# An eight-core linear attention and FFN kernel: the transposed tile is copied out of PSUM by VectorE instead of ScalarE, and the two large weights are loaded last

## The chip, the cores and the metric
The kernel runs on 8 cores of one Trainium2 chip, four on each die. Every core runs the same program on its own sequence. The time is device microseconds of the slowest core. Three runs of the kernel before are shown; the profile is of one further execution.

## The reference
The input x has 8 sequences of 4096 tokens with 1024 values. One core has one sequence.

```
xn = layernorm(x)
# attention: 8 heads of 64, phi(u) = elu(u) + 1, gamma = sigmoid(decay_log)
q, k = phi(xn @ W_Q.T), phi(xn @ W_K.T);  v = xn @ W_V.T
S = gamma*S + k v^T;  z = gamma*z + k         # over the tokens
y = (S^T q) / (z.q + 1e-6) * sigmoid(xn @ W_g.T + b)
s = y @ W_O.T
# spiking FFN
h = relu(xn @ W_fc.T)**2;  y = h @ W_proj.T   # 4096 wide
mem = 0; five times: reset = mem > 1
    mem = 0.9*mem + y - reset;  spikes += mem > 1
out = x + s * silu(spikes / 5)
```

## The kernel before
**Tiles.** A sequence is cut into 32 chunks of 128 tokens, and two chunks make a supertile; there are 16. All weights stay in SBUF as bf16. The normalised and transposed input of a supertile lies in `XR`: 1024 values in eight blocks of 128 rows, and in each block the 128 columns of chunk 0 and those of chunk 1.

**Order.** Each engine runs a program that is written out in order, with semaphore waits between the engines. `Eng.op` puts a drain ahead of an operation that reads or writes what an earlier one of its engine has written since the last drain (or writes what one has read); it does so by the name of the tile. TensorE's program has no drains. `inc` marks the operations that others can wait for.

**A supertile.** For each of its two chunks TensorE makes q in PSUM bank pb2 (L423), k in pb3, the gate in pb2 and v in pb3, then the attention products; VectorE and ScalarE do the element work between them. During this GpSimd loads the x tile that comes two chunks later (`load_xt`), and `emit_A_stats` forms its sums on ScalarE (L298 to L304) and its mean and deviation on GpSimd. Then comes the FFN: 32 blocks of fc products into pb2 or pb3, relu on ScalarE (L661), squaring on VectorE (L666), pj products into pb4, pb5, pb0 and pb1. Then the output projection of chunk 0 into pb2 and pb3.

**The spikes.** `spike_group` handles two of the four banks of y. The even bank's five threshold steps are Sign operations of ScalarE (L747), the odd bank's five are comparisons on VectorE (L752); TensorE adds them up with identity products, even and odd in turn. ScalarE then takes a Tanh of either sum (L781), and VectorE makes the gate out of it (L786, L790).

**Around the change.** The end of a supertile is issued in this order:

```python
        spike_group(0, 1)
        wo1_doh0()
...
            emit_A_xn(c0 + 2, 0)     # place A
        spike_group(2, 3)
        wo1_doh1()
        if sti + 1 < nst:
            emit_A_xn(c0 + 3, 1)     # place B
...
        emit_combine(0, c0, xg_st, spk_s_tail, spk_g_tail)
```

`emit_A_xn` prepares a chunk of the next supertile: ScalarE normalises the x tile into `XF` (L366), TensorE transposes it in eight blocks into the PSUM tile `pbT` (L374), and eight copies of 128 columns bring it into `XR` (L382). The two calls are named place A and place B here; the last supertile has neither. `emit_combine` multiplies s (in pb2 and pb3 for chunk 0) by the gate on VectorE (L809), adds x on GpSimd (L818) and stores. The same for chunk 1 is put off into the next supertile. The q projection of a supertile's first chunk waits for the multiplications of the chunk two before, which read pb2 and pb3:

```python
                E_pe.wait(E_v, combine_mul[c0 - 2])
                E_pe.wait(E_s, xnte_done.get(ch, 0))
```

**The start.** GpSimd issues the loads of all weights, f32 in HBM and bf16 in SBUF, fc and pj (8 MB each in SBUF) ahead of four projections and wo (1 MB each), and the first two x tiles after them. SP issues ten small loads of constants. ScalarE and VectorE work out decay masks from the constants. TensorE's first projection waits for all seven weights.

Of the kernel before, what the change touches and what calls it, by code (L numbers as in the profile page):

```python
# [8 lines left out]
AF = mybir.ActivationFunctionType  # L9
# [3 lines left out]
P = 128  # L13
# [5 lines left out]
CH = 128  # L19
# [70 lines left out]
def build_program(T):  # L90
# [7 lines left out]
    wq_d = dt_("wq", [P, 8 * FH], F32, kind="ExternalInput").ap()  # L98
    wk_d = dt_("wk", [P, 8 * FH], F32, kind="ExternalInput").ap()
    wv_d = dt_("wv", [P, 8 * FH], F32, kind="ExternalInput").ap()  # L100
    wg_d = dt_("wg", [P, 8 * FH], F32, kind="ExternalInput").ap()
    wo_d = dt_("wo", [P, 4 * D], F32, kind="ExternalInput").ap()
    fc_d = dt_("fc", [P, 8 * FF], F32, kind="ExternalInput").ap()
    pj_d = dt_("pj", [P, 32 * D], F32, kind="ExternalInput").ap()
# [13 lines left out]
    wq = S_("wq_sb", [P, 8 * FH], BF16)  # L118
    wk = S_("wk_sb", [P, 8 * FH], BF16)
# [59 lines left out]
                            tile_position=tp)  # L179
        return E_pe.op(f, reads=reads, writes=writes, inc=inc)  # L180

    for w_sb, w_dr in [(fc, fc_d), (pj, pj_d), (wq, wq_d), (wk, wk_d),
                       (wv, wv_d), (wg, wg_d)]:
        E_gp.dma(w_sb[:], w_dr, "wt")
    E_gp.dma(wo[:], wo_d, "wt")

    for dst, src in [(identb[:], identb_d), (tsc, tsc_d), (zmask, zmask_d),
                     (r1t, r1_d), (r127[:], r127_d), (sel[:], sel_d),
# [83 lines left out]
                scalar1=G128B[r_ * DKH:(r_ + 1) * DKH, h:h + 1]),  # L272
                reads=("SCRB", "G128B"), writes=("GDEC",), inc=(p_ == 3 and r_ == 1))

    E_pe.wait(E_gp, ("wt", 7), dma=True)
    E_pe.wait(E_v, c_ssb0)

    xt_cnt = {}
# [80 lines left out]
    def emit_A_xn(ch, cc):  # L359
        buf = XT[ch % 2]  # L360
        key = f"XT{ch % 2}"
        st_ = stats
        rcol = 8 if ch % 2 == 0 else 14
        ncol = 9 if ch % 2 == 0 else 15
        E_s.wait(E_gp, xnstat_done[ch])
        c_xn = E_s.op(lambda e, b=buf, rcol=rcol, ncol=ncol: e.activation(  # L366
            XF[:], b[:], AF.Identity, scale=st_[:, rcol:rcol + 1],
            bias=st_[:, ncol:ncol + 1]),
            reads=(key, "stats"), writes=("XF",), inc=True)
        xnact_done[ch] = c_xn  # L370
        gp_guard["s"] = c_xn
        E_pe.wait(E_s, c_xn)
        for dk in range(8):
            c_T = E_pe.op(lambda e, dk=dk: e.transpose(pbT[:, dk * P:(dk + 1) * P],  # L374
                                                       XF[:, dk * P:(dk + 1) * P],
                                                       identb[:]),
                          reads=("XF", "identb"), writes=("pbT",), inc=(dk == 7))
        xntp_done[ch] = c_T
        E_s.wait(E_pe, c_T)
        for dk in range(8):  # L380
            col = dk * (ST * CH) + cc * CH
            c_ev = E_s.op(lambda e, dk=dk, col=col: e.activation(  # L382
                XR[:, col:col + CH], pbT[:, dk * P:(dk + 1) * P], AF.Identity),
                reads=("pbT",), writes=("XR",), inc=(dk == 7))
        xnte_done[ch] = c_ev

    load_xt(0)
    load_xt(1)
# [22 lines left out]
    for sti in range(nst):  # L411
        c0 = sti * ST
        chunks = [c0, c0 + 1]
        for cc, ch in enumerate(chunks):
            qbank, kbank = pb[2], pb[3]
            if cc == 0:
                E_pe.wait(E_v, combine_mul[c0 - 2])
                E_pe.wait(E_s, xnte_done.get(ch, 0))
            else:
                E_pe.wait(E_s, th_done[ch - 1])  # L420
                E_pe.wait(E_v, vaug_done[ch - 1])
                E_pe.wait(E_s, xnte_done.get(ch, 0))
            for ft in range(4):  # L423
                for dk in range(8):
                    c_qps = mm(qbank[:, ft * P:(ft + 1) * P],
# [115 lines left out]
                          reads=("QF",), writes=("ZP",), inc=True)  # L541
            E_pe.wait(E_v, c_at)
            if cc == 0:
                E_pe.wait(E_s, xnte_done.get(ch + 1, 0))
            for ft in range(4):
                c_kt = E_pe.op(lambda e, ft=ft: e.transpose(
                    pbT[:, ft * P:(ft + 1) * P], KF[:, ft * P:(ft + 1) * P],
# [96 lines left out]
        def emit_fc(ft):  # L644
            bank = pb[2 + ft % 2]
            E_pe.wait(E_v, h2_cnt.get(ft - 2, 0))
            if ft == 0:
                E_pe.wait(E_s, th_c1)
                E_pe.wait(E_v, vaug_c1)
            for dk in range(8):  # L650
                c_fc = mm(bank[:, 0:ST * CH],
                          fc[:, dk * FF + ft * P:dk * FF + (ft + 1) * P],
                          XR[:, dk * ST * CH:(dk + 1) * ST * CH],
                          start=(dk == 0), stop=(dk == 7),
                          reads=("fc_sb", "XR"), writes=(f"pb{2 + ft % 2}",),
                          inc=(dk == 7))
            fc_cnt[ft] = c_fc
            E_s.wait(E_pe, c_fc)
            E_s.wait(E_pe, pj_cnt.get(ft - 2, 0))
            relu_cnt[ft] = E_s.op(  # L660
                lambda e, b=bank, ft=ft: e.activation(H2[ft % 2][:], b[:, 0:ST * CH],  # L661
                                                      AF.Relu),
                reads=(f"pb{2 + ft % 2}",), writes=(f"H2_{ft % 2}",), inc=True)
            E_v.wait(E_s, relu_cnt[ft])
            h2_cnt[ft] = E_v.op(
                lambda e, b=bank, ft=ft: e.tensor_tensor(  # L666
                    out=H2[ft % 2][:], in0=H2[ft % 2][:], in1=b[:, 0:ST * CH],
                    op=ALU.mult),
                reads=(f"H2_{ft % 2}", f"pb{2 + ft % 2}"),
                writes=(f"H2_{ft % 2}",), inc=True)  # L670

        def emit_pj(ft):
# [12 lines left out]
                              inc=(tsub == ST - 1 and doh == 1))  # L685
            pj_cnt[ft] = c_pj

        emit_fc(0)
        emit_fc(1)
        for ft in range(1, 32):  # L690
# [269 lines left out]
```

How the kernel before makes its waits and increments, by code:

```python
            def run(e, fn=fn):  # L52
                fn(e).then_inc(me.sem, 1)
# [17 lines left out]
        def run(e, d=dst_ap, s=src_ap, key=key):  # L71
            e.dma_start(out=d, in_=s).then_inc(me.dsem[key], 16)
# [3 lines left out]
    def wait(self, other, value, dma=False):  # L76
        if dma:
            key, n = value
            if n <= 0:
                return
            o = other
            self.prog.append(lambda e: e.wait_ge(o.dsem[key], n * 16))
        else:
            if value <= 0:
                return
            o = other
            self.prog.append(lambda e: e.wait_ge(o.sem, value))
```

## Time and profile before

| | us |
|---|---|
| runs | 2083.9, 2088.89, 2091.3 (median 2088.89) |
| the profiled execution | 2091.03 |
| its span on the slowest core (core 3) | 2089.5 |
| spans of the eight cores | 2067.4 to 2089.5 |
| TensorE busy | 1552.3 (74%) |
| VectorE busy | 755.5 (36%) |
| ScalarE busy | 668.6 (32%) |
| GpSimd busy | 253.9 (12%) |

The mean granted clock of TensorE was 0.884 on core 3 and 0.884 to 0.893 over the cores. The span runs from the first to the last instruction of a core. In the profile PE is TensorE, PEld its weight loads, DVE VectorE, ACT ScalarE, POOL GpSimd and SP SyncE; a q behind a name is the queue that issues. All products that go through the helper `mm` have the line L178, and are told apart by their tiles. A supertile takes about 119.5 us.

### The profile page before, as it was taken

Reading aid. Unit: us, or ns where it says so; the run is one execution under the profiler, and the core shown is the slowest. Engines: PE = TensorE matmul, PEld = TensorE weight load, DVE = VectorE, ACT = ScalarE, POOL = GpSimd, SP = SyncE. Lnnn points to the kernel's source line nnn. Section 1 sums busy time; section 2 is a strip of 40 time slices with the busy share of each in tenths; the row PEclk is TensorE's granted clock in tenths of the full one; section 3 lists DMA queues with packets and bytes.
Section 4 is the critical chain, followed back from the end, with each engine's and each line's share of the span. In section 5 each row is a group of like instructions: output and inputs, shape, how many; then the busy total and the mean of one; then the engine's idle time right before and its main releaser. Section 6 shows DMA issues by size and latency. Waiting matters only on the chain.

```text
span 2089.5 us, 35959 instructions; the slowest of 8 cores (2067.4 to 2089.5 us)
## 1 busy us (share of the span) xinstructions
PE 1552.3 (74%) x12130; PEld 1035.1 (50%) x12130; DVE 755.5 (36%) x1576; ACT 668.6 (32%) x1497; POOL 253.9 (12%) x843
## 2 busy tenths in 40 slices
PE   0005969778796968779696977879697877969695
PEld 0004646455564646455464645456464645546462
DVE  0013243343425243343524344342534334342433
ACT  0024242423324242432424242332424243242422
POOL 1002011020202011020201102020201102020100
PEclk9998979989898988889798988979798888979898
DMA  9980010010201010010201001020101001020100
GB/s 146 158 131 11 1 36 6 18 24 1 42 1 37 6 33 10 6 37 1 42 1 36 6 20 23 1 41 1 36 6 32 10 6 36 1 42 1 36 1 26
DMA packets 16294, 58.03 MB, mean 28 GB/s; under 512 B 2667, under 2 KB 2676, under 8 KB 14964
## 3 DMA queue, kind: packets, MB, share of 16 engines
q0 software_dynamic: 10480, 38.80, 12.3%
q1 hardware_dynamic: 5636, 16.92, 2.4%
q8 instruction: 103, 1.69, 0.3%
q14 instruction: 75, 0.61, 0.1%
HBM read 77.74 MB, written 16.78 MB: 45 GB/s over the span
## 4 chain that ended last, share of the span: by engine, by line
PE 64%; DVE 9%; ACT 9%; another core or an unknown queue 6%; issue 6%; DVEq 4%; DMA 1%; POOLq 1%; ACTq 1%; POOL 0%; SPq 0%
PE pb L178 63%; DVEq L38 3%; ACT XR L382 2%; DVE MEM L809 2%; ACT SGN L781 1%; ACT SGN L747 1%; ACT XF L366 1%; DVE AT L529 1%; DVE KF L462 1%; DVE VT L502 1%; ACT SCRB L458 1%; ACT KF L456 1%; DVE MEM L786 1%; POOLq L38 1%
## 5 line engine op out<-in xcount | busy, mean ns | idle before, releaser
L178 PE MATMUL pb<-XR,fc_sb 128*128 128x256 bf16 x4096 | 556.4, 282 | 0.0
L178 PE MATMUL pb<-pj_sb,H 128*128 128x512 bf16 x2048 | 536.4, 385 | 5.8 <-DVE H L666 5.7
L178 PEld LDWEIGHTS pb<-XR,fc_sb 128*128 128x128 bf16 x4096 | 413.0, 101 | 164.7 <-issue 5.8
L666 DVE TENSOR_TENSOR H<-H,pb 128x256 bf16<-128x256 bf16 x512 | 215.7, 421 | 666.2 <-ACT H L661 665.2
L661 ACT ACTIVATE H<-pb 128x256 bf16<-128x256 f32 x512 | 196.2, 383 | 738.9 <-PE pb L178 738.9
L178 PEld LDWEIGHTS pb<-pj_sb,H 128*128 128x128 bf16 x2048 | 201.6, 99 | 153.0 <-issue 22.6
L72 POOL DMA_DIRECT2D XF<-x_tok x32 | 18.8, 588 | 1104.2 <-PE pbT L374 1095.1
L178 PE MATMUL pb<-SGN,identb_sb 128*128 128x512 bf16 x192 | 85.2, 496 | 87.2 <-ACT SGN L747 82.0
L178 PE MATMUL pb<-XR,wq_sb 128*128 128x128 bf16 x1024 | 108.8, 302 | 38.4 <-DVE MEM L809 29.9
L178 PEld LDWEIGHTS pb<-XR,wq_sb 128*128 128x128 bf16 x1024 | 101.8, 143 | 41.6 <-issue 40.5
L298 ACT ACTIVATE XF<-XT 128x1024 bf16<-128x1024 bf16 x32 | 33.8, 1056 | 221.9 <-DMA XT<-x_tok 213.2
L818 POOL TENSOR_TENSOR MEM<-MEM,XF 128x512 f32<-128x512 f32 x64 | 74.3, 1162 | 248.5 <-DVE MEM L809 127.4
L752 DVE TENSOR_SCALAR SGN<-pb 128x512 bf16<-128x512 f32 x96 | 66.3, 690 | 81.2 <-PE pb L178 78.2
L178 PEld LDWEIGHTS pb<-SGN,identb_sb 128*128 128x128 bf16 x192 | 19.1, 100 | 150.9 <-issue 150.5
L178 PE MATMUL pb<-lgn,onesr_sb 1*128 1x8 f32 x2 | 0.6, 352 | 121.6 <-ACT lgn L202 121.6
L374 PE MATMUL pbT<-identb_sb,XF 128*128 128x128 bf16 x256 | 20.2, 224 | 87.4 <-ACT XF L366 87.4
L382 ACT ACTIVATE XR<-pbT 128x128 bf16<-128x128 bf16 x256 | 70.9, 277 | 43.9 <-PE pbT L374 28.0
L178 PE MATMUL pb<-XR,wk_sb 128*128 128x128 bf16 x1024 | 81.0, 252 | 0.0
L442 DVE SCALAR_TENSOR_TENSOR QF<-pb,SCRB 128x512 bf16<-128x512 f32 x32 | 22.1, 692 | 157.8 <-ACT SCRB L438 157.8
L178 PEld LDWEIGHTS pb<-XR,wk_sb 128*128 128x128 bf16 x1024 | 78.2, 118 | 0.0
L178 PE MATMUL pb<-wv_sb,XR 128*128 128x512 bf16 x256 | 60.4, 378 | 13.1 <-DVE KF L462 13.1
L178 PE MATMUL pb<-XR,wg_sb 128*128 128x128 bf16 x1024 | 62.3, 219 | 7.3 <-DVE QF L442 7.0
(127 smaller groups left out, 1569.1 us busy)
## 6 DMA issues: line engine op xcount, KB each, us to landing
out<-MEM SPq DMA_DIRECT2D x32, 512.0 KB, 3.3
fc_sb<-fc POOLq DMA_DIRECT2D x1, 8192.0 KB, 58.8
pj_sb<-pj POOLq DMA_DIRECT2D x1, 8192.0 KB, 112.2
XT<-x_tok POOLq DMA_DIRECT2D x32, 256.0 KB, 4.4
XF<-x_tok POOLq DMA_DIRECT2D x32, 256.0 KB, 4.6
wq_sb<-wq POOLq DMA_DIRECT2D x1, 1024.0 KB, 117.8
wk_sb<-wk POOLq DMA_DIRECT2D x1, 1024.0 KB, 123.4
wv_sb<-wv POOLq DMA_DIRECT2D x1, 1024.0 KB, 128.9
```

The source lines that it names most:

```text
L38: self.prog.append(lambda e: e.drain())
L178: return e.matmul(out_ap, lhsT_ap, rhs_ap, start=start, stop=stop, tile_position=tp)
L298: E_s.op(lambda e, b=buf: e.activation(XF[:], b[:], AF.Identity, accum_out=st_[:, 0:1]), reads=(key,), writes=("XF",))
L366: c_xn = E_s.op(lambda e, b=buf, rcol=rcol, ncol=ncol: e.activation(XF[:], b[:], AF.Identity, scale=st_[:, rcol:rcol + 1], bias=st_[:, nco ...
L382: c_ev = E_s.op(lambda e, dk=dk, col=col: e.activation(XR[:, col:col + CH], pbT[:, dk * P:(dk + 1) * P], AF.Identity), reads=("pbT",), wri ...
L442: c_qf = E_v.op(lambda e: e.scalar_tensor_tensor(out=QF[:], in0=qbank[:, 0:FH], scalar=0.0, in1=SCRB[:], op0=ALU.max, op1=ALU.add), reads= ...
L456: E_s.op(lambda e: e.activation(KF[:], kbank[:, 0:FH], AF.Relu, scale=-1.0), reads=("pb3",), writes=("KF",))
L661: lambda e, b=bank, ft=ft: e.activation(H2[ft % 2][:], b[:, 0:ST * CH], AF.Relu),
L666: lambda e, b=bank, ft=ft: e.tensor_tensor(out=H2[ft % 2][:], in0=H2[ft % 2][:], in1=b[:, 0:ST * CH], op=ALU.mult),
L752: vc = E_v.op(lambda e, bufO=bufO, j=j, c=cO: e.tensor_scalar(out=bufO[:, 0:FH], in0=pb[c["bk"]][:, 0:FH], scalar1=THS[j], scalar2=2.0, op ...
L809: c_mul = E_v.op(lambda e, doh=doh, cc=cc, sb_=sb_: e.tensor_tensor(out=OUTB[:, doh * FH:(doh + 1) * FH], in0=sb_[:, 0:FH], in1=G[:, cc * ...
L818: c_comb = E_gp.op(lambda e, doh=doh: e.tensor_tensor(out=OUTB[:, doh * FH:(doh + 1) * FH], in0=OUTB[:, doh * FH:(doh + 1) * FH], in1=XF[: ...
```

## The change
The eight copies of `emit_A_xn` become `tensor_copy` on VectorE, at the same point of the order. ScalarE no longer waits for the transposes; VectorE does. Two waits are added: ScalarE waits for the last transposes before it writes `XF` again, and TensorE waits for VectorE's last copies before it transposes into `pbT` again. TensorE's waits for a finished `XR` name VectorE. At the start fc and pj are issued after the other five weights, still ahead of the x tiles, and count on a semaphore of their own; TensorE's first projection waits for five weights, and the first fc product for these two.

```diff
--- before.py
+++ after.py
@@ -179,10 +179,11 @@
                             tile_position=tp)
         return E_pe.op(f, reads=reads, writes=writes, inc=inc)
 
-    for w_sb, w_dr in [(fc, fc_d), (pj, pj_d), (wq, wq_d), (wk, wk_d),
-                       (wv, wv_d), (wg, wg_d)]:
+    for w_sb, w_dr in [(wq, wq_d), (wk, wk_d), (wv, wv_d), (wg, wg_d)]:
         E_gp.dma(w_sb[:], w_dr, "wt")
     E_gp.dma(wo[:], wo_d, "wt")
+    E_gp.dma(fc[:], fc_d, "wt2")
+    E_gp.dma(pj[:], pj_d, "wt2")
 
     for dst, src in [(identb[:], identb_d), (tsc, tsc_d), (zmask, zmask_d),
                      (r1t, r1_d), (r127[:], r127_d), (sel[:], sel_d),
@@ -272,7 +273,7 @@
                 scalar1=G128B[r_ * DKH:(r_ + 1) * DKH, h:h + 1]),
                 reads=("SCRB", "G128B"), writes=("GDEC",), inc=(p_ == 3 and r_ == 1))
 
-    E_pe.wait(E_gp, ("wt", 7), dma=True)
+    E_pe.wait(E_gp, ("wt", 5), dma=True)
     E_pe.wait(E_v, c_ssb0)
 
     xt_cnt = {}
@@ -363,6 +364,7 @@
         rcol = 8 if ch % 2 == 0 else 14
         ncol = 9 if ch % 2 == 0 else 15
         E_s.wait(E_gp, xnstat_done[ch])
+        E_s.wait(E_pe, gp_guard.get("tp", 0))
         c_xn = E_s.op(lambda e, b=buf, rcol=rcol, ncol=ncol: e.activation(
             XF[:], b[:], AF.Identity, scale=st_[:, rcol:rcol + 1],
             bias=st_[:, ncol:ncol + 1]),
@@ -370,19 +372,22 @@
         xnact_done[ch] = c_xn
         gp_guard["s"] = c_xn
         E_pe.wait(E_s, c_xn)
+        E_pe.wait(E_v, gp_guard.get("te", 0))
         for dk in range(8):
             c_T = E_pe.op(lambda e, dk=dk: e.transpose(pbT[:, dk * P:(dk + 1) * P],
                                                        XF[:, dk * P:(dk + 1) * P],
                                                        identb[:]),
                           reads=("XF", "identb"), writes=("pbT",), inc=(dk == 7))
         xntp_done[ch] = c_T
-        E_s.wait(E_pe, c_T)
+        gp_guard["tp"] = c_T
+        E_v.wait(E_pe, c_T)
         for dk in range(8):
             col = dk * (ST * CH) + cc * CH
-            c_ev = E_s.op(lambda e, dk=dk, col=col: e.activation(
-                XR[:, col:col + CH], pbT[:, dk * P:(dk + 1) * P], AF.Identity),
+            c_ev = E_v.op(lambda e, dk=dk, col=col: e.tensor_copy(
+                out=XR[:, col:col + CH], in_=pbT[:, dk * P:(dk + 1) * P]),
                 reads=("pbT",), writes=("XR",), inc=(dk == 7))
         xnte_done[ch] = c_ev
+        gp_guard["te"] = c_ev
 
     load_xt(0)
     load_xt(1)
@@ -415,11 +420,11 @@
             qbank, kbank = pb[2], pb[3]
             if cc == 0:
                 E_pe.wait(E_v, combine_mul[c0 - 2])
-                E_pe.wait(E_s, xnte_done.get(ch, 0))
+                E_pe.wait(E_v, xnte_done.get(ch, 0))
             else:
                 E_pe.wait(E_s, th_done[ch - 1])
                 E_pe.wait(E_v, vaug_done[ch - 1])
-                E_pe.wait(E_s, xnte_done.get(ch, 0))
+                E_pe.wait(E_v, xnte_done.get(ch, 0))
             for ft in range(4):
                 for dk in range(8):
                     c_qps = mm(qbank[:, ft * P:(ft + 1) * P],
@@ -541,7 +546,7 @@
                           reads=("QF",), writes=("ZP",), inc=True)
             E_pe.wait(E_v, c_at)
             if cc == 0:
-                E_pe.wait(E_s, xnte_done.get(ch + 1, 0))
+                E_pe.wait(E_v, xnte_done.get(ch + 1, 0))
             for ft in range(4):
                 c_kt = E_pe.op(lambda e, ft=ft: e.transpose(
                     pbT[:, ft * P:(ft + 1) * P], KF[:, ft * P:(ft + 1) * P],
@@ -685,6 +690,8 @@
                               inc=(tsub == ST - 1 and doh == 1))
             pj_cnt[ft] = c_pj
 
+        if sti == 0:
+            E_pe.wait(E_gp, ("wt2", 2), dma=True)
         emit_fc(0)
         emit_fc(1)
         for ft in range(1, 32):
```

## Rows read from the trace of the kernel before

**Rows 1.** The page: the chain that ended last, shares of the span by engine.
```profile
PE 64%; DVE 9%; ACT 9%; another core or an unknown queue 6%; issue 6%; DVEq 4%; DMA 1%; POOLq 1%; ACTq 1%; POOL 0%; SPq 0%
```

**Rows 2.** The list of waits, whole span: who waited for whom, us in total, times, longest.
```profile
PE pb L178 <- DVE MEM L809: 37.1, 27, 2.8
...
PE pb L178 <- ACT XR L382: 8.4, 3, 2.8
```

**Rows 3.** Timeline, eleventh supertile, place A: start us, us, engine, line, operation, [idle before <-releaser].
```profile
1468.93 0.61 PE L374 MATMUL pbT<-identb_sb,XF 128*128 128x128 bf16 x8 [1.41 <-ACT XF L366]
1469.50 0.69 DVE L790 SCALAR_TENSOR_TENSOR G<-SGN,MEM 128x512 bf16<-128x512 bf16 x1
1469.63 2.69 ACT L382 ACTIVATE XR<-pbT 128x128 bf16<-128x128 bf16 x8 [0.85 <-PE pbT L374]
1470.29 0.69 DVE L752 TENSOR_SCALAR SGN<-pb 128x512 bf16<-128x512 f32 x1
...
1473.25 1.01 PE L178 MATMUL pb<-SGN,identb_sb 128*128 128x512 bf16 x2 [3.72 <-ACT SGN L747]
...
1477.38 1.26 ACT L781 ACTIVATE SGN<-pb,CONSTC 128x512 bf16<-128x512 f32 x2 [1.02 <-PE pb L178]
```

**Rows 4.** Timeline, eleventh supertile, place B.
```profile
1479.92 0.61 PE L374 MATMUL pbT<-identb_sb,XF 128*128 128x128 bf16 x8 [1.29 <-ACT XF L366]
1480.49 0.69 DVE L790 SCALAR_TENSOR_TENSOR G<-SGN,MEM 128x512 bf16<-128x512 bf16 x1
1480.62 2.69 ACT L382 ACTIVATE XR<-pbT 128x128 bf16<-128x128 bf16 x8 [0.85 <-PE pbT L374]
...
1481.28 1.46 DVE L809 TENSOR_TENSOR MEM<-pb,G 128x512 f32<-128x512 f32 x2
...
1482.99 3.57 PE L178 MATMUL pb<-XR,wq_sb 128*128 128x128 bf16 x32 [2.46 <-DVE MEM L809]
```

**Rows 5.** Timeline, place B of the second and of the fifteenth supertile.
```profile
406.12 2.69 ACT L382 ACTIVATE XR<-pbT 128x128 bf16<-128x128 bf16 x8 [0.85 <-PE pbT L374]
...
408.49 2.81 PE L178 MATMUL pb<-XR,wq_sb 128*128 128x128 bf16 x32 [2.46 <-DVE MEM L809]
...
1957.99 2.69 ACT L382 ACTIVATE XR<-pbT 128x128 bf16<-128x128 bf16 x8 [0.85 <-PE pbT L374]
...
1960.35 2.93 PE L178 MATMUL pb<-XR,wq_sb 128*128 128x128 bf16 x26 [2.46 <-DVE MEM L809]
```

**Rows 6.** Groups of instructions (busy us, mean ns, idle before) and a line of the timeline.
```profile
L594 DVE COPY SCRB<-pbT 8x128 bf16<-8x128 bf16 x32 | 6.8, 213 | 16.6 <-PE pbT L590 16.6
...
130.88 1.13 DVE L252 TENSOR_TENSOR DMASK<-DMASK,G 128x128 bf16<-128x128 bf16 x4 [4.93 <-ACT DMASK L235]
```

**Rows 7.** Timeline, last supertile, second spike group.
```profile
2065.86 0.69 DVE L752 TENSOR_SCALAR SGN<-pb 128x512 bf16<-128x512 f32 x1
...
2070.29 1.26 ACT L781 ACTIVATE SGN<-pb,CONSTC 128x512 bf16<-128x512 f32 x2 [1.23 <-PE pb L178]
```

**Rows 8.** DMA issues of the first 160 us: KB each, median us from issue to landing.
```profile
pj_sb<-pj POOLq DMA_DIRECT2D x1, 8192.0 KB, 112.2
...
XT<-x_tok POOLq DMA_DIRECT2D x2, 256.0 KB, 142.0
```

**Rows 9.** Timeline of the start.
```profile
119.36 1.28 ACT L196 ACT_TABLE_LOAD   x1 [119.36 <-DMA dls<-dl]
...
147.48 1.06 ACT L298 ACTIVATE XF<-XT 128x1024 bf16<-128x1024 bf16 x1 [15.01 <-DMA XT<-x_tok]
...
207.13 3.59 PE L178 MATMUL pb<-XR,fc_sb 128*128 128x256 bf16 x16
```

**Rows 10.** DMA queues from 10 to 110 us: packets, MB, share of 16 engines.
```profile
q0 software_dynamic: 494, 15.66, 99.3%
q1 hardware_dynamic: 494, 0.04, 0.7%
```

**Rows 11.** Engines by stretch: PE, PEld, DVE, ACT, POOL busy, granted clock, DMA share, GB/s.
```profile
1484.00:1486.00 2.00, 2.00 (x22) 2.00 (x20) 0.00 (x0) 0.00 (x0) 0.33 (x1) 0.50 0.47 86
```

## The prediction
> **What bounds the kernel now.** I read the page first for the whole: a chain that ended last that is made up of TensorE for 64% and of VectorE and ScalarE for 9% each [rows 1]. So TensorE sets the time while the fc and pj products run, and what stands between two such stretches is a chain through all three engines. The change touches nothing inside the fc and pj loop. It touches the start (order of loads) and two places in each supertile but the last, 15 supertiles with two places each. So I read the list of waits next, for who holds TensorE up: 27 of its idle stretches before a product, 37.1 us, end with the two multiplications of L809 on VectorE, and three, 8.4 us, are put down to the copies of L382 on ScalarE [rows 2]. Then the timeline around both places of one supertile, the eleventh.
>
> Place A lies between the two spike groups [rows 3]. The eight transposes start at 1468.93. ScalarE copies the result out from 1469.63 to 1472.32, and only then begins its Sign steps; TensorE, which must take the even step first, waits until 1473.25. VectorE meanwhile does its odd step from 1470.29 and is idle when the even product starts. The reader is to see that ScalarE holds place A up, not VectorE.
>
> Place B lies after the second group [rows 4]. Transposes at 1479.92; ScalarE copies from 1480.62 to 1483.31; VectorE ends the gate products at 1481.18 and starts the combine multiplications 0.10 us later, until 1482.74; TensorE starts the q projection of the next supertile at 1482.99. That is before the last ScalarE copy has ended. It is so in 11 of the 15 supertiles, as the second shows (products at 408.49, copies done at 408.81) and the fifteenth (1960.35 against 1960.68) [rows 5]. What TensorE waits for here is pb2 and pb3, which L809 reads; the columns that it projects first were copied at place A. The three waits that the list puts on L382 I take for coincidences of an end with a start; the code has no such wait for the copies of this place. So at place B the ScalarE copies cost nothing now, and VectorE is the one that holds the next supertile up.
>
> **The copies at place B.** The changed VectorE program has, between the gate product and the multiplications, a wait and eight copies with seven drains between them (each writes XR, which the one before has written). Price of one: the nearest row is L594, a bf16 copy of 128 columns out of the same PSUM tile, 213 ns [rows 6] (on 8 partitions instead of 128; across the rows of VectorE it is columns that the time goes with). With a drain between them, four operations of 128 columns of 226 ns take 1.13 us [rows 6], a pitch of (1.13 - 0.23)/3 = 0.30, that is 0.075 beyond the duration. Pitch of a copy: 0.213 + 0.075 = 0.288; eight: 2.30 us. The far bound is what ScalarE needs for the same copy, 2.69/8 = 0.336 each, plus a drain that is dearer than ScalarE's: say the 2.69 us again with 0.1 for the wait, 2.8 us. The near bound is the eight durations with nothing between them, 8 x 0.213 = 1.70. I take 2.30, the row that is nearest. The transposes end at 1480.54, before VectorE is free, so the new wait for them is empty. All of it lies on the path: the multiplications start 2.30 later, and the q projection with them. Behind the waiting TensorE stands the whole next supertile; nothing later waits for a fixed time that could swallow the shift.
>
> The Trainium skill (VectorE: DVE Perf Modes, Specifications) says that VectorE sits closer to SBUF and ScalarE closer to PSUM, which speaks against this move; by it a copy would cost VectorE no less than ScalarE. Were it so in time, place B would cost 2.8 instead of 2.3. The row says otherwise: 213 ns, against 0.336 us from copy to copy on ScalarE. The same page (Why PSUM operands drop a tier) caps a copy out of PSUM at two elements per cycle, and its table gives 192 ns at that rate and 258 at one element per cycle for 128 columns, an estimate; the row lies near the first.
>
> **The copies at place A.** VectorE's gate product ends at 1470.19 (1469.50 + 0.69). Then come the same eight copies, so its first odd step starts at 1470.29 + 2.30 = 1472.59. ScalarE, freed, takes its first Sign right after the normalisation, so the even product is issued while the copies run and TensorE then waits for the odd one. How long from the first odd step to the Tanh that ends the group, when ScalarE is ahead in this way? The last supertile has no copies and shows just this order: first odd step 2065.86, Tanh 2070.29, 4.43 us [rows 7]. That puts the Tanh at 1477.02, against 1477.38 now: 0.36 gained. Counted another way, by TensorE's own queue at the half clock: the odd operand is ready at 1472.59 + 0.69 = 1473.28, its product 0.25 later as at place B, 1473.53; now it is the second of the pair at 1473.25, 0.38 behind it, 1473.63; the eight that follow keep the pitch they have; gain 0.10. I take 0.30, nearer to the row that shows the order itself. Below, it can be nothing or a loss of 0.3 (copies at 2.8 us); above, 0.9, if TensorE held its full clock through the group: the 4.13 us from the even product to the Tanh would then shrink to the five Sign steps of 0.69 of one engine, 3.45, some 0.6 more.
>
> **The waits that are added.** TensorE waits for VectorE's last copies before it transposes again, ScalarE for TensorE's last transposes before it overwrites XF. Both were done a whole place earlier (11 us), so they cost nothing but their issue. The normalised tile's other waits name VectorE instead of ScalarE, for values long reached.
>
> **The order of the loads.** fc and pj, 8 MB each in SBUF, were first in the GpSimd queue and now come after the four projections and wo. The x tiles are issued behind all of them, before and after. They landed 142.0 us after issue, pj after 112.2 [rows 8], and ScalarE started on x at 147.48 after 15.01 us of idleness [rows 9]. One queue lands in order of issue, and the bytes ahead of x are the same, so x lands at the same time, and the first products with it: gain nothing. What the move frees, TensorE's wait for five weights in place of seven, ended before x in any case. The new wait for fc and pj stands before the product of 207.13 [rows 9], 60 us after they land. The constants on SP's queue landed at 119.36 [rows 9]: from 10 to 110 us that queue moved 494 packets beside 494 of GpSimd's [rows 10], one for one. With the smaller packets of the projections first, the constants will be there some 80 us sooner; their setup ended before x came already, so this gives nothing either. If they landed with x instead, ScalarE's setup (147.48 - 15.01 - 119.36 = 13.1 us) would be on the path; nothing speaks for it. For the changed mix of packets ahead of x I leave 3 us either way.
>
> At the start both normalised tiles pass through VectorE, which is idle there: nothing.
>
> **Sum.** 15 x (2.30 - 0.30) = 30.0 us. The profiled execution took 2091.03 us (span 2089.5 and what lies around it), 2.1 over the median of the runs shown, 2088.89. On the median: 2118.9, so 2119.
>
> **Rivals.**
> Early start: the x tiles land with the first weights, at some 50 us. Then the first supertile's attention, from the landing to 207.13 about 60 us, hides under the load of fc and pj, and the fc product starts at about 147. That saves up to 60 us, and with 30 lost the time is about 2059. It turns the sign once x lands over 30 us sooner. Against it: the order of landings in [rows 8]. Chance 3%.
> Full clock: TensorE restarts at place B at half clock, 0.50 (1.2 GHz) in 1484 to 1486 [rows 11], after 2.5 us of idleness. If the new order kept it at 2.4 GHz through group and projections, the 32 q products of 3.57 us would take half, 1.8 less, and place A would give its 0.9: 2.7 saved for 2.3 lost, 6 us gained in all, 2083, just past what can be told. It decides where more than 2.3 is saved. Against it: at B the idleness grows to 4.7 us. Chance 2%. The Trainium skill (TensorE: Matmul & The Clock Gate, Part 1: The HAM clock gate) says that the array runs at full rate only after sustained work; this speaks against it too.
> Hidden copies: TensorE is not released by L809 at place B, or the two engines' order lets the copies pass beside it; then only A's gain is left, 15 x 0.3 = 4.5, 2084 to 2089, no change that can be told. For it: three waits put down to L382. Against it: 11 of 15 starts before those copies end. Chance 4%.
> Dear copies: 2.8 us or more at B and a loss of 0.3 at A: 15 x 3.1 = 46, 2135. Chance 11%.
> The forecast has 80%.
>
> **Numbers.** A measurement of this kernel can tell about 0.3%, 6 us. The forecast's own range: copies of 1.9 us with 0.9 gained at A give 15 us, the copies of 2.8 without gain 42. With the 3 us of the start and the scatter of the runs, 2106 to 2133; this leaves out the first three rivals and the upper end of the fourth, under 2 in 10. Slower: 80 + 11 = 91%. Within 0.3%: 4%. Faster: 3 + 2 = 5%.
>
> **What the profile after would show.** L382's line as 256 VectorE copies of about 213 ns. At place B eight of them between gate product and multiplications, 2.2 to 2.4 us, and the wait of TensorE for L809 up from 37 to about 70 us. At place A the first even product before the copies end, the Tanh 0.2 to 0.4 us sooner after the transposes. x landing near 147 us, constants before 45, the first fc product unmoved. I am wrong if x lands early, if the copies are over 0.35 us apart, or if place B's start does not move with them.

## The result, and the profile after

The changed kernel is slower: over 13 runs of each the ratio is 1.0086, with a 95% interval of 1.0066 to 1.0105. That is 18 us on 2088.9; 30 were forecast. The median is 2107.9 us, but six of the 13 runs were disturbed and the ratio leaves them out; the other seven took 2104.2 to 2107.9 us, four of them below the forecast's range of 2106 to 2133. The profiled execution took 2106.99 us (span 2105.5, core 7).

The page of the changed kernel: its first line, the engines' busy time, the chain that ended last, and the group of the copies.

```profile
span 2105.5 us, 36008 instructions; the slowest of 8 cores (2098.5 to 2105.5 us)
...
PE 1541.0 (73%) x12130; PEld 1031.5 (49%) x12130; DVE 806.1 (38%) x1832; ACT 600.0 (28%) x1241; POOL 253.1 (12%) x843
...
PE 62%; DVE 14%; another core or an unknown queue 6%; issue 6%; ACT 6%; DVEq 5%; POOLq 1%; ACTq 0%; DMA 0%; POOL 0%
...
L386 DVE COPY XR<-pbT 128x128 bf16<-128x128 bf16 x256 | 57.4, 224 | 108.5 <-PE pbT L377 90.7
```

Beside [rows 1] the chain has passed from ScalarE (9% to 6%) to VectorE (9% to 14%). The 256 copies are now VectorE's, 224 ns each.

The list of waits, as in [rows 2]:

```profile
PE pb L178 <- DVE MEM L816: 73.7, 30, 4.6
...
PE pb L178 <- DVE SGN L759: 48.7, 18, 3.4
...
PE pb L178 <- ACT SGN L754: 25.4, 21, 1.8
```

L816 is L809 of before. TensorE waited 37.1 us for it, and now 73.7; the waits put down to the copies are gone.

The timeline of place A in the eleventh supertile, to be laid beside [rows 3]:

```profile
1478.04 0.61 PE L377 MATMUL pbT<-identb_sb,XF 128*128 128x128 bf16 x8 [1.52 <-ACT XF L368]
...
1478.51 0.69 DVE L797 SCALAR_TENSOR_TENSOR G<-SGN,MEM 128x512 bf16<-128x512 bf16 x1
...
1478.91 0.38 PE L178 MATMUL pb<-SGN,identb_sb 128*128 128x512 bf16 x1 [0.27 <-issue]
1479.12 2.02 DVE L386 COPY XR<-pbT 128x128 bf16<-128x128 bf16 x7
...
1481.44 0.23 DVE L386 COPY XR<-pbT 128x128 bf16<-128x128 bf16 x1 [0.31 <-issue]
1481.59 0.68 DVE L759 TENSOR_SCALAR SGN<-pb 128x512 bf16<-128x512 f32 x1
...
1482.63 0.58 PE L178 MATMUL pb<-SGN,identb_sb 128*128 128x512 bf16 x1 [3.34 <-DVE SGN L759]
...
1486.33 1.27 ACT L788 ACTIVATE SGN<-pb,CONSTC 128x512 bf16<-128x512 f32 x2 [1.02 <-PE pb L178]
```

The even product (1478.91) no longer waits for the copies; TensorE now waits for the odd one (1482.63), which stands behind the copies on VectorE. From the transposes to the Tanh it took 8.29 us here, against 8.45 in [rows 3]. In this supertile A to B shrank by only 0.06 us (from 10.99 to 10.93); the mean over all is in the table below.

The timeline of place B, beside [rows 4]:

```profile
1488.97 0.61 PE L377 MATMUL pbT<-identb_sb,XF 128*128 128x128 bf16 x8 [1.05 <-ACT XF L368]
1489.44 0.69 DVE L797 SCALAR_TENSOR_TENSOR G<-SGN,MEM 128x512 bf16<-128x512 bf16 x1
1490.05 2.30 DVE L386 COPY XR<-pbT 128x128 bf16<-128x128 bf16 x8
...
1492.44 1.46 DVE L816 TENSOR_TENSOR MEM<-pb,G 128x512 f32<-128x512 f32 x2
...
1494.15 2.08 PE L178 MATMUL pb<-XR,wq_sb 128*128 128x128 bf16 x18 [4.57 <-DVE MEM L816]
```

This is the loss, drawn out: gate product until 1490.13, eight copies from 1490.05 to 1492.35, multiplications from 1492.44, the q projection 5.18 us after the transposes instead of 3.07. TensorE does nothing between 1489.58 and 1494.15.

The start: landings, and two lines of the timeline of ScalarE and one of TensorE, beside [rows 8, 9].

```profile
fc_sb<-fc POOLq DMA_DIRECT2D x1, 8192.0 KB, 88.6
pj_sb<-pj POOLq DMA_DIRECT2D x1, 8192.0 KB, 140.1
...
XT<-x_tok POOLq DMA_DIRECT2D x2, 256.0 KB, 141.0
```

```profile
58.83 1.28 ACT L197 ACT_TABLE_LOAD   x1 [58.83 <-DMA dls<-dl]
...
146.49 1.06 ACT L299 ACTIVATE XF<-XT 128x1024 bf16<-128x1024 bf16 x1 [74.53 <-DMA XT<-x_tok]
...
206.49 3.59 PE L178 MATMUL pb<-XR,fc_sb 128*128 128x256 bf16 x16
```

x lands at the time it did (141.0 us after issue instead of 142.0), although the constants are there 60 us sooner and wo, the last of the five weights, landed 37.4 us after issue instead of 140.9. The first fc product is unmoved. (I had put the constants before 45 us; it was 58.8.)

**Where the time went.** The stretches between four events of each supertile, read from the timelines of all eight cores and averaged over 15 supertiles (from fc to the next A over 14), in us. A and B are the starts of the transposes, q the first q product, fc the first fc product. The period is from one B to the next.

| kernel | A to B | B to q | q to fc | fc to A | period |
|---|---|---|---|---|---|
| before | 11.02 | 3.16 | 37.10 | 67.66 | 118.93 |
| changed | 10.79 | 5.17 | 37.08 | 67.30 | 120.34 |
| difference | -0.23 | +2.01 | -0.02 | -0.36 | +1.41 |

Fifteen times 1.41 is 21.2 us. The remaining difference from the 18 measured lies between the cores. In 17 runs of the kernel before that accompanied the first experiments, the slowest core stood 5.6 us above the mean of the eight; in eight runs of the changed kernel (the seven above and one more), 2.9 us. The time is that of the slowest core, so 2.7 us of the loss do not show. The mean core of the same runs lost 20.9 us (2080.6 to 2101.5), as the table has it. In two later sets of six runs of the kernel before the distance was 5.2 and 4.7 us, so the 2.7 is known to about half a microsecond.

**The stretch from fc to A.** Nothing in it was changed, and it became 0.36 us shorter. The view of engines by stretch shows why, here in a pair of stretches that stand far apart. Of the kernel before, the 8 us after the first fc product of the tenth supertile (clock in the third column from the end):

```profile
1281.11:1289.11 8.00, 8.00 (x45) 5.16 (x42) 3.27 (x7) 1.15 (x3) 4.29 (x22) 0.66 0.01 3
```

Of the changed kernel, the same stretch:

```profile
1290.40:1298.40 8.00, 7.94 (x53) 5.32 (x50) 3.69 (x8) 1.54 (x4) 4.30 (x22) 0.85 0.00 1
```

After the attention part TensorE enters the FFN at half clock (the granted clock is 0.50, 1.2 GHz, in the 2 us before the first fc product), and some time later the full clock is granted. In these two stretches the mean was 0.66 and 0.85, with 45 and 53 products begun. Over eight cores and 14 supertiles each, the mean is 0.704 before and 0.755 after: 0.051 x 8 us = 0.41 us of full clock more, about the 0.36 (or 0.46, if the 0.10 by which the transposes now start later is taken out). From then on both run at 1.00. How the earlier grant comes about was not isolated; no edit touches this stretch. It is no scatter: the loads alone gave 67.67 us at a clock of 0.707, as before, and the copies alone 67.30 at 0.757. Nor does the longer pause at place B decide it: with one ScalarE copy in the kernel before, B to q stayed 3.16 us, and yet the stretch took 67.33 us at 0.746.

### The profile page after: what moved, and what is told of

Its sections match the earlier page's. It is cut to its first block, busy times and chain, and to the rows that moved or that the text cites. A ratio compares the mean times of both kernels' runs of the same rounds, so it can differ in the third digit from the quotient of the medians.

```text
span 2105.5 us, 36008 instructions; the slowest of 8 cores (2098.5 to 2105.5 us)
## 1 busy us (share of the span) xinstructions
PE 1541.0 (73%) x12130; PEld 1031.5 (49%) x12130; DVE 806.1 (38%) x1832; ACT 600.0 (28%) x1241; POOL 253.1 (12%) x843
## 4 chain that ended last, share of the span: by engine, by line
PE 62%; DVE 14%; another core or an unknown queue 6%; issue 6%; ACT 6%; DVEq 5%; POOLq 1%; ACTq 0%; DMA 0%; POOL 0%
PE pb L178 62%; DVEq L38 5%; DVE MEM L793 2%; DVE XR L386 2%; DVE MEM L816 2%; DVE KF L467 1%; ACT SGN L788 1%; DVE AT L534 1%; DVE VT L507 1%; ACT SCRB L463 1%; ACT KF L461 1%; ACT SGN L754 1%; DVE SGN L759 1%; POOLq L38 1%
## 5 line engine op out<-in xcount | busy, mean ns | idle before, releaser
L178 PE MATMUL pb<-pj_sb,H 128*128 128x512 bf16 x2048 | 530.7, 382 | 6.0 <-DVE H L671 5.7
L178 PE MATMUL pb<-XR,wq_sb 128*128 128x128 bf16 x1024 | 113.1, 310 | 68.5 <-DVE MEM L816 68.5
L386 DVE COPY XR<-pbT 128x128 bf16<-128x128 bf16 x256 | 57.4, 224 | 108.5 <-PE pbT L377 90.7
L377 PEld LDWEIGHTS pbT<-identb_sb,XF 128*128 128x128 bf16 x256 | 15.4, 99 | 166.1 <-issue 166.1
L551 PE MATMUL pbT<-identb_sb,KF 128*128 128x128 bf16 x128 | 13.3, 231 | 80.4 <-DVE AT L534 80.4
L441 ACT ACTIVATE QF<-pb 128x512 bf16<-128x512 f32 x32 | 19.1, 597 | 180.2 <-PE pb L178 180.2
```

The costliest lines, as they stand in the source:

```text
L178: return e.matmul(out_ap, lhsT_ap, rhs_ap, start=start, stop=stop, tile_position=tp)
L386: c_ev = E_v.op(lambda e, dk=dk, col=col: e.tensor_copy(out=XR[:, col:col + CH], in_=pbT[:, dk * P:(dk + 1) * P]), reads=("pbT",), writes= ...
```

## The experiments

Each ratio is to the kernel before, on the same chip, with its 95% interval.

**Copies alone, loads in their old order.**

```diff
-    for w_sb, w_dr in [(wq, wq_d), (wk, wk_d), (wv, wv_d), (wg, wg_d)]:
+    for w_sb, w_dr in [(fc, fc_d), (pj, pj_d), (wq, wq_d), (wk, wk_d),
+                       (wv, wv_d), (wg, wg_d)]:
...
-    E_gp.dma(fc[:], fc_d, "wt2")
-    E_gp.dma(pj[:], pj_d, "wt2")
...
-    E_pe.wait(E_gp, ("wt", 5), dma=True)
+    E_pe.wait(E_gp, ("wt", 7), dma=True)
...
-        if sti == 0:
-            E_pe.wait(E_gp, ("wt2", 2), dma=True)
```

> The changed kernel with the loads in their old order (fc and pj first, one semaphore). Theory: the load order is worth nothing, so this stands where the changed kernel stands, ratio to the kernel before 1.007 to 1.010, multiplications at place B 2.0 us later after the transposes (3.47 instead of 1.36 to 1.71). Rival: the new load order gave back part of what the copies cost, then this is slower than the changed kernel by what it gave, ratio 1.012 to 1.015.

Measured: 1.0095 (1.0068 to 1.0123), and a table row like the changed kernel's (10.78, 5.17, 37.07, 67.30). The copies alone make the whole loss.

**Loads alone**, the same edit the other way round on the kernel before, with the wait for fc and pj ahead of the first fc product.

> The kernel before with only the loads reordered; the copies stay on ScalarE. Theory: within 0.3% of the kernel before; x lands at 139 to 149 us on every core as before, only the constants are earlier. Rival: the load order is worth 3 to 12 us either way (ratio 0.994 to 0.998, or 1.002 to 1.006), with x landing earlier or later by as much.

Measured: 0.9992 (0.9975 to 1.0009). Nothing, as forecast.

**Multiplications first.** The copies of place B are emitted after `emit_combine`; with `later=True`, `emit_A_xn` hands them back as a function.

```diff
...
-            emit_A_xn(c0 + 3, 1)
+            copies_B = emit_A_xn(c0 + 3, 1, later=True)
...
         emit_combine(0, c0, xg_st, spk_s_tail, spk_g_tail)
+        if sti + 1 < nst:
+            copies_B()
```

> The changed kernel, but at place B VectorE does the two combine multiplications before the eight copies. Theory: the whole loss is these copies ahead of the multiplications; q projection again 3.1 us after the transposes, place A keeps its gain of 0.23 us: 18 to 26 us less than the changed kernel, ratio to the kernel before 0.995 to 0.999. Rival: the copies cost through something else (the shared PSUM tile, the clock, VectorE being fuller): then half or more of the loss stays, ratio 1.004 or above.

Measured: 0.9971 (0.9952 to 0.9990). Its timeline at place B of the same supertile (L388 are the copies, L821 the multiplications):

```profile
1468.98 0.61 PE L377 MATMUL pbT<-identb_sb,XF 128*128 128x128 bf16 x8 [1.09 <-ACT XF L368]
1469.44 0.69 DVE L802 SCALAR_TENSOR_TENSOR G<-SGN,MEM 128x512 bf16<-128x512 bf16 x1
...
1470.23 1.46 DVE L821 TENSOR_TENSOR MEM<-pb,G 128x512 f32<-128x512 f32 x2
1471.60 2.31 DVE L388 COPY XR<-pbT 128x128 bf16<-128x128 bf16 x8
...
1471.94 3.57 PE L178 MATMUL pb<-XR,wq_sb 128*128 128x128 bf16 x32 [2.35 <-DVE MEM L821]
```

The copies take the same 2.31 us, now beside the q projection, and TensorE starts 2.96 us after the transposes. The order of two pieces of work on one engine was worth 1.15%; the rival (the PSUM tile, VectorE's load) is out.

**Place A on VectorE, place B back on ScalarE.** The waits for the finished copies follow the engine.

```diff
...
-        E_v.wait(E_pe, c_T)
+        on_v = True if cc == 0 else False
+        E = E_v if on_v else E_s
+        E.wait(E_pe, c_T)
...
+            if on_v:
+                f = lambda e, dk=dk, col=col: e.tensor_copy(
+                    out=XR[:, col:col + CH], in_=pbT[:, dk * P:(dk + 1) * P])
+            else:
+                f = lambda e, dk=dk, col=col: e.activation(
+                    XR[:, col:col + CH], pbT[:, dk * P:(dk + 1) * P], AF.Identity)
...
```

> The changed kernel with place B's copies back on ScalarE; place A's stay on VectorE. Theory: nothing of the loss is left, and place A's gain stays, ratio 0.995 to 0.999, as in the run with the multiplications first. Rival: moving place A's copies costs by itself, then this is at or above 1.001 and differs from that run.

Measured: 0.9960 (0.9942 to 0.9978); A to B 10.64, B to q 2.98. Place A's move alone gains.

**Place B's copies twice.** The second eight write the same values again.

```diff
-        for dk in range(8):
+        seq = list(range(8)) * (2 if cc == 1 and ch > 1 else 1)
+        for n, dk in enumerate(seq):
...
```

> The changed kernel with place B's eight copies made twice (16 copies; the second eight write the same values). Theory: what stands ahead of the multiplications is paid in full: 8 x 0.288 = 2.30 us more at place B, 15 x 2.3 = 35 us more than the changed kernel, ratio to the kernel before 1.022 to 1.027. Rival: part of any delay at place B comes back later in the supertile, as some 0.37 us of the first 2.0 seem to have done in the stretch from the first fc product to place A: then 24 to 31 us more, ratio 1.020 or less.

Measured: 1.0287 (1.0262 to 1.0311), above what either expected. B to q is 7.65, 2.48 us more than the changed kernel, where 8 x 0.288 had been counted (the sixteen copies take 4.78 us, the eight of the changed kernel 2.31); fc to A is 67.45, 0.15 more than in the changed kernel, and the period 122.91, 2.57 more, 15 times 38.6. So the delay is paid in full, and what fc to A had given is partly gone: the 0.36 is no share of the delay that comes back, and the rival falls.

**One copy in place of eight**, at both places.

```diff
-        for dk in range(8):
-            col = dk * (ST * CH) + cc * CH
-            c_ev = E_v.op(lambda e, dk=dk, col=col: e.tensor_copy(
-                out=XR[:, col:col + CH], in_=pbT[:, dk * P:(dk + 1) * P]),
-                reads=("pbT",), writes=("XR",), inc=(dk == 7))
+        XR3 = XR[:].rearrange("p (k c) -> p k c", c=ST * CH)
+        pT3 = pbT[:].rearrange("p (k c) -> p k c", c=P)
+        c_ev = E_v.op(lambda e: e.tensor_copy(
+            out=XR3[:, :, cc * CH:(cc + 1) * CH], in_=pT3),
+            reads=("pbT",), writes=("XR",), inc=True)
```

> The changed kernel with one VectorE copy of 8 x 128 columns in place of eight copies, at both places. Theory: what costs is the fixed part of each copy and the drains between them; one copy of 1024 columns takes about 0.7 us (425 ns for 512 columns, 0.55 ns per column more), 1.6 less than 2.31, at both places: place B's multiplications 1.85 us after the transposes, 1.6 saved at A too, up to 48 us less than the changed kernel, ratio 0.984 to 0.990. Rival: the columns cost, one copy takes 1.1 us or more (1.04 ns per column) and the strided output slows it: ratio 0.992 or above.

Measured: 0.9878 (0.9854 to 0.9902). Place B in its timeline:

```profile
1456.68 0.61 PE L377 MATMUL pbT<-identb_sb,XF 128*128 128x128 bf16 x8 [1.01 <-ACT XF L368]
...
1457.76 0.68 DVE L386 COPY XR<-pbT 128x1024 bf16<-128x1024 bf16 x1
...
1458.54 1.46 DVE L816 TENSOR_TENSOR MEM<-pb,G 128x512 f32<-128x512 f32 x2
...
1460.25 3.57 PE L178 MATMUL pb<-XR,wq_sb 128*128 128x128 bf16 x32 [2.96 <-DVE MEM L816]
```

One copy of 1024 columns takes 0.68 us against 2.30 for eight of 128. A to B is 9.07, B to q 3.61.

**The same on ScalarE**, in the kernel before, with nothing moved: one `activation` over the same two views.

> The kernel before with one ScalarE copy of 8 x 128 columns in place of eight, at both places. Theory: at place A ScalarE holds the group up, so what one copy saves there (2.69 down to about 1.1 us) is gained, 15 x 1.6 = 24 us; at place B nothing, as its copies cost nothing: ratio 0.987 to 0.990, about as the run with one VectorE copy, without any work moved. Rival: VectorE's multiplications or its odd steps take over at place A and less than half is gained: ratio 0.994 or above.

Measured: 0.9852 (0.9832 to 0.9873). Its group of copies, from the list of groups:

```profile
L382 ACT ACTIVATE XR<-pbT 128x1024 bf16<-128x1024 bf16 x32 | 32.8, 1024 | 27.9 <-PE pbT L374 27.9
```

1.02 us instead of 2.69; A to B is 9.36 and B to q 3.16 as before. ScalarE is dearer per copy than VectorE (1.02 against 0.68 us) and the result is as good, since place B stays free. It gained somewhat more than the 24 us expected: A to B fell by 1.66 us, as counted, and fc to A by 0.33.

**The first x tiles ahead of fc and pj.** The two loads of x further down go.

```diff
...
     E_gp.dma(wo[:], wo_d, "wt")
...
+    for ch in range(2):
+        xt_cnt[ch] = E_gp.dma(XT[ch][:], x_tok_d[ch], f"xt{ch}")
     E_gp.dma(fc[:], fc_d, "wt2")
...
-    load_xt(0)
-    load_xt(1)
...
```

> The changed kernel with the first two x tiles issued right behind wo, ahead of fc and pj. Theory: the order of the queue alone kept x at 147 us; now x lands near 43 us, the first q product stands near 67 us, the second chunk is held by the x tile of chunk 2, which lands behind pj (ScalarE waits for it in order), so the first fc product comes near 168 instead of 207: 35 to 40 us less than the changed kernel, ratio 0.989 to 0.993. Rival: something else holds the start (the constants, the setup), then the gain is under 15 us.

Measured: 1.0086 (1.0068 to 1.0104), just the changed kernel's: no gain. The theory fell. x had landed, from the view of DMA issues:

```profile
XT<-x_tok POOLq DMA_DIRECT2D x2, 256.0 KB, 39.1
```

and ScalarE had summed it by 58 us. Then GpSimd's timeline:

```profile
6.07 0.79 POOL L72 DMA_DIRECT2D pj_sb<-pj  x1
57.80 0.22 POOL L314 TENSOR_SCALAR stats<-stats 128x1 f32<-128x1 f32 x1 [50.94 <-ACT XF L308]
147.72 0.21 POOL L317 TENSOR_SCALAR stats<-stats 128x1 f32<-128x1 f32 x1 [89.70 <-issue]
```

Between the first two operations of the statistics there is a drain, and it lasted until 147.7. pj had landed at 6.07 + 141.1 = 147.2.

**The drain by itself.** Two memsets on GpSimd ahead of its loads, and two between the load of pj and those of x; all four write the tile GPT, so each but the first has a drain ahead of it.

```diff
...
+    for n in range(2):
+        E_gp.op(lambda e, n=n: e.memset(GPT[:, n:n + 1], 1.0), writes=("GPT",))
     for w_sb, w_dr in [(wq, wq_d), (wk, wk_d), (wv, wv_d), (wg, wg_d)]:
...
     E_gp.dma(pj[:], pj_d, "wt2")
+    for n in range(2, 4):
+        E_gp.op(lambda e, n=n: e.memset(GPT[:, n:n + 1], 1.0), writes=("GPT",))
```

> The changed kernel with four tiny memsets on GpSimd: two ahead of its first load with a drain between them, two behind the last load with a drain between them. Theory (a drain waits for the issued transfers): the first pair is under 1 us apart; of the second pair the first runs near 7 us and the second only when the x tiles or the weights have landed, after 140 us. Rival: the drain waits for nothing of the kind; both pairs are under 1 us apart, and x's tiles are issued at 8 us.

Its timeline of GpSimd:

```profile
1.06 0.31 POOL L184 MEMSET GPT<- 128x1 f32 x2 [0.38 <-POOLq L94]
...
5.26 0.77 POOL L72 DMA_DIRECT2D pj_sb<-pj  x1
141.75 0.31 POOL L191 MEMSET GPT<- 128x1 f32 x2 [135.71 <-issue]
142.42 1.09 POOL L72 DMA_DIRECT2D XT<-x_tok  x2 [0.36 <-issue]
```

The first pair runs at once. The second pair runs at 141.75, both of them, since the drain ahead of the third was already there; pj landed at 5.26 + 136.1 = 141.4. So GpSimd's drain waits for the transfers it has issued, here and in the run before. Whether it waits for the landing itself, or for some work of GpSimd on these transfers that ends with them, these runs do not tell apart.

**Early x, and the statistics of the first two chunks on VectorE.**

```diff
...
+        g = E_v if ch < 2 else E_gp
...
-        E_gp.wait(E_s, c_sq)
-        E_gp.wait(E_s, gp_guard["s"])
-        g = E_gp
+        g.wait(E_s, c_sq)
+        g.wait(E_s, gp_guard["s"])
...
```

> The run with the early x tiles, and the mean and deviation of the first two chunks worked out on VectorE instead of GpSimd. There x landed 39 us after issue, but GpSimd stood still from 58.02 to 147.72 between two operations that have a drain between them, just until pj had landed. Theory: GpSimd's drain waits for the transfers that it has issued; with the statistics on VectorE the first q product comes near 72 us and the first fc product near 170, 30 to 40 us less than the changed kernel, ratio 0.989 to 0.995. Rival: something else holds the start until pj lands (the weights' semaphore, the queue); then no gain, ratio 1.007 or above.

Measured: 0.9911 (0.9893 to 0.9929), 1.75% under the changed kernel's ratio, 37 us. The first q product and the point at which ScalarE gets chunk 2's tile, which it awaits in order ahead of chunk 1:

```profile
76.70 3.62 PE L178 MATMUL pb<-XR,wq_sb 128*128 128x128 bf16 x32
```

```profile
149.78 1.06 ACT L304 ACTIVATE XF<-XT 128x1024 bf16<-128x1024 bf16 x1 [62.01 <-DMA XT<-x_tok]
```

The first chunk's attention is now under the load; the second still waits for pj, which landed at 6.07 + 142.3 = 148.4. GpSimd issued chunk 2's load at 69.80, with pj in flight: in the run before, the drain had held GpSimd up, and not the issuing.

**All together.** Early x, one copy, multiplications first; and the same with the statistics on VectorE.

> The changed kernel with the first two x tiles ahead of fc and pj, one copy instead of eight at both places, and the multiplications ahead of the copy at place B. Theory: the three add up: 37 us at the start, 15 x 1.6 at place A, 15 x 2.1 at place B: about 90 us less than the changed kernel, ratio 0.963 to 0.970. Rival: they overlap, at place A another step (the gate product, the Sign chain) takes over and the gain there is under 0.8: ratio 0.972 or above.

Measured: 0.9811 (0.9788 to 0.9834), not the 0.963 to 0.970 expected, since the start gained nothing. The number lies where the rival had it, but not for its reason: A to B is 9.13 and B to q 3.01, so places A and B gained 1.66 and 2.16 us, as the theory had it.

> The run with all three edits (early x, one copy, multiplications first) and the statistics of the first two chunks on VectorE. Theory: that run gained nothing at the start; with GpSimd's drain out of the way it gains 30 to 40 us more: ratio 0.961 to 0.967. Rival: as above, no more than 0.978.

Measured: 0.9635 (0.9606 to 0.9664), the profiled execution 2008.1 us: faster than both kernels, by 3.7% and 4.5%.

## Why the prediction was right in its sign and too large in its size

- **The steps that failed, in short.** The direction and the path were right. Of the 12 us between 30 and 18, 5.4 are the stretch from the first fc product to place A, which the sum put at nothing; 4.4 are place B, sized at 2.30 where 2.01 was measured; 2.7 are the spread of the cores. Place A, which gained 0.07 less than forecast, goes the other way by 1.1.
- **Place B, the mechanism: right.** The copies stand between the gate product and the multiplications, and TensorE waits for these. Copies alone, multiplications first, and the copies twice show it.
- **Place B, the size: 2.30 forecast, 2.01 measured.** The eight copies took 2.30 to 2.31, as counted, though not by its parts: each takes 224 ns instead of 213 and they start 0.297 apart instead of 0.288, and I had counted eight steps where there are seven and one copy. What was mis-sized is the surroundings: in four of the 15 supertiles of before the multiplications came 0.44 us after the gate product instead of 0.09, and this gap is gone behind the copies; the first copy starts 0.08 before the product ends; and the transposes, with two waits ahead of them, start 0.10 us later beside the gate product (it ends 1.16 us after their start, 1.26 in [rows 3, 4]), which the table counts ahead of A and not behind B. 15 x 0.29 = 4.4 us too much. The last of the three is a shift of the mark and no time: counted from the end of the gate product place B lost 2.12 us, and the stretch from fc to A gained 0.46.
- **Place A: 0.30 forecast, 0.23 measured.** Right within a tenth; the row of the last supertile had given 0.36, TensorE's queue 0.10. 1.1 us too little gained. Two errors stand against each other in it: on average the first odd step came 0.13 us sooner than counted (3.42 us after the transposes, which themselves start 0.10 later, against 3.66), and from there to the Tanh it took 4.72 us, not the 4.43 of the last supertile.
- **What is missing in the sum: the clock at the start of the FFN, 0.36 us a supertile, 5.4 us.** I had let the clock into the range only at places A and B. "The change touches nothing inside the fc and pj loop" was true of the code and not of the time. The step that failed is the sum's silence on this stretch: it put it at nothing, and it gave 0.36 us back at each supertile, with a mean clock of 0.755 instead of 0.704 in its first 8 us. Why the clock came earlier stays open.
- **The slowest core.** I added a shift that every core has to the time of the slowest one. The spread fell by 2.7 us. Together: 30.0 - 4.4 + 1.1 - 5.4 - 0.3 (q to fc) = 21.0, against 21.2 from the periods; less 2.7 it is 18.3, against 18 measured. The interval of the ratio is 4 us wide to either side, so that it fits so closely is in part luck.
- **The range.** Its own terms give a wider one: 2088.9 + 15 - 3 = 2101 at the lower end, and 2088.9 + 42 + 3 = 2134 at the upper. I set the lower end at 2106 without a reason, and four of the seven runs fell below it.
- **The waits that are added.** I said that they cost nothing but their issue. The transposes start 0.25 us after the end of the normalisation, and 0.14 in the kernels whose TensorE lacks the wait for the last copies (before, the loads alone, one copy on ScalarE). Nothing on the path waits for these 0.10 us: at both places the copies begin when VectorE is through with the gate product.
- **Loads: worth nothing, right, but for half the reason.** I gave the order of the queue as the reason, and the time of the early start, once x landed with the first weights, as 2059. With x at 44 us nothing was gained: behind the queue stood a second hold, GpSimd's drain. With both out of the way the gain was 37 us, not 60, because chunk 2's tile holds the second chunk.
- **VectorE's copy against ScalarE's.** The Trainium skill (VectorE: DVE Perf Modes, Specifications) says that ScalarE sits closer to PSUM. In time this did not decide here: 224 ns on VectorE against 277 on ScalarE for 128 columns, 0.68 us against 1.02 for 1024. The Trainium skill's cap of two elements per cycle out of PSUM (VectorE: DVE Perf Modes, Why PSUM operands drop a tier), with the clock of 0.96 GHz in its Specifications, makes 896 more columns cost 0.47 us, an estimate. The rows agree: 0.68 - 0.22 = 0.46.
- **The rivals.** Hidden copies, full clock and dear copies are out. The three waits that the list had put down to L382 were coincidences: with those copies on ScalarE and one of them 1.7 us shorter (one copy on ScalarE), B to q stayed 3.16.

## What to carry to other kernels

Before work is moved to an engine that is idle on average, look at what that engine does next at that point, and who waits for it; here the same move gained at one place and lost almost nine times as much at the other, and swapping two pieces of work on the engine would have kept the gain. Eight small copies with drains between them are mostly fixed cost: making them one was worth more than any choice of engine. And when a wait is removed, ask what stands behind it before giving it a price: the early x tile was held a second time.

## What the runs showed of the hardware that I had not expected

- A drain on GpSimd waits for the transfers that GpSimd has issued: ahead of a memset that has nothing to do with them until 141.75, some 0.4 us after the last had landed, while a pair of memsets with a drain between them and nothing in flight took 0.31 us.
- In a stretch that no edit touches the full clock came earlier, with 0.755 against 0.704 in its first 8 us on average, worth 0.36 us a supertile. The length of TensorE's pause at place B, 40 us earlier, does not decide it by itself: with that pause as before (one ScalarE copy, B to q 3.16) the clock was 0.746 and fc to A 67.33; with it slightly shorter (multiplications first, 2.96) 0.718 and 67.59; with it 2.5 us longer than in the changed kernel (copies twice, 7.65) 0.732 and 67.45. What does was not settled.
